# Four-stage gated cross-attention and mixture-of-experts kernel: a later store in one DMA queue, and products of a stage placed ahead of the work before them

## The reference, cut to what matters

```python
x = x + tanh(g_xattn[0]) * softmax_attention(_layernorm(x), ctx)      # stage A: 32 heads, masks
x = x + tanh(g_ffn[0])   * bitlinear_ffn(_layernorm(x))               # stage B: ternary weights
x = x + tanh(g_xattn[1]) * linear_attention(_layernorm(x), ctx)       # stage C: phi(q), phi(k), gate, Wo
x = x + tanh(g_ffn[1])   * moe(_layernorm(x))                         # stage D

# moe(x):
shared = (silu(x @ sw1.T) * (x @ sw2.T)) @ sw3.T                      # 2048 hidden
scores = sigmoid(x @ router_w.T)                                      # 8 experts, the top 2 of each token
h1, h2 = split(x @ w12[e].T); out_e = (silu(h1) * h2) @ w3[e].T       # 256 hidden in each expert
return shared + sum over the two experts of (weight * out_e)
```

## Time and profile before

| what | us |
| --- | --- |
| three runs: median (lowest to highest) | 1779.1 (1773.74 to 1786.65) |
| the profiled execution | 1774.64 |
| its span, first to last instruction | 1772.9 |
| PE busy in the span | 1594.1 (90%) |
| DVE, POOL, ACT busy | 967.4, 824.5, 711.1 |
| stage D's first PE product | at 1046.11 |
| routed stage on PE | 1497.17 to 1703.52 |
| mean granted TensorE clock | 0.969 of full speed |

### The profile page before, as it was taken

One profiled execution on the slowest core, in us unless ns is written; L12 is line 12 of the kernel. 1 busy time (PEld: TensorE's weight loads), 2 busy tenths in 40 slices (PEclk: granted clock), 3 DMA queues, 4 the chain that ended last, 5 costly groups with the idle time before them and its releaser, 6 DMA issues. The chain is left out here.

```text
span 1772.9 us, 29275 instructions
## 1 busy us (share of the span) xinstructions
PE 1594.1 (90%) x10826; PEld 829.7 (47%) x10826; DVE 967.4 (55%) x1947; ACT 711.1 (40%) x1311; POOL 824.5 (47%) x853
## 2 busy tenths in 40 slices
PE   4589999999848999979999979999999998888898
PEld 3246665665423444426565634444444443333343
DVE  5556666767547999834656443467543333111137
ACT  3178888888935556522233221211111111222211
POOL 2388887878843455433444245335433520111134
PEclk9899999999769999989999989999999999999999
DMA  5644544323414555443553437446544641565746
GB/s 165 163 103 108 114 94 109 95 66 67 115 27 91 120 116 108 83 89 70 96 123 81 93 84 161 99 101 135 127 102 101 154 88 36 147 158 145 153 134 192
DMA packets 453939, 195.68 MB, mean 110 GB/s; under 512 B 395484, under 2 KB 418270, under 8 KB 453800
## 3 DMA queue, kind: packets, MB, share of 16 engines
q1 hardware_dynamic: 448120, 175.19, 44.3%
q0 software_dynamic: 5680, 18.62, 4.1%
HBM read 77.17 MB, written 22.81 MB: 56 GB/s over the span
## 5 line engine op out<-in xcount | busy, mean ns | idle before, releaser
L1020 POOL TENSOR_TENSOR a_pl<-a_prob,a_ph 128x512 f16<-128x512 f32 x256 | 295.1, 1166 | 73.8 <-ACT a_prob L928 73.2
L1103 DVE TENSOR_REDUCE a_mx<-bank 128x2 f32<-128x512 f32 x256 | 173.0, 686 | 101.0 <-PE bank L652 99.2
L140 PE MATMUL bank<-XTh,d_whs 128*128 128x512 f16 x512 | 194.1, 379 | 3.2 <-PEq L89 2.3
L142 PE MATMUL bank<-XTh,d_wls 128*128 128x512 f16 x512 | 194.0, 379 | 0.0
L141 PE MATMUL bank<-XTl,d_whs 128*128 128x512 f16 x512 | 194.0, 379 | 0.0
L927 ACT ACTIVATE a_ph<-bank 128x512 f16<-128x512 f32 x256 | 153.9, 601 | 59.8 <-PE bank L672 32.0
L2225 POOL CAST d_cut<-d_raw 128x512 f16<-128x512 f32 x90 | 56.8, 631 | 228.3 <-DMA d_raw<-in_L_ffn_sw 147.9
L928 ACT ACTIVATE a_prob<-bank 128x512 f32<-128x512 f32 x256 | 154.3, 603 | 0.0
L2145 DVE TENSOR_TENSOR d_hid<-d_hid,bank 128x512 f32<-128x512 f32 x64 | 43.9, 686 | 175.4 <-PE bank L142 162.1
L2237 POOL DMA_INDIRECT e_x<-rows,d_who x39 | 37.1, 951 | 190.8 <-DMA e_xTl<-e_x 184.8
L2136 ACT ACTIVATE d_hid<-bank 128x512 f32<-128x512 f32 x64 | 38.2, 597 | 211.2 <-PE bank L142 211.2
(11 more groups left out here) (330 smaller groups left out, 3997.7 us busy)
## 6 DMA issues: line engine op xcount, KB each, us to landing
d_raw<-in_L_ffn_w SPq DMA_DIRECT2D x48, 256.0 KB, 3.0
d_raw<-in_L_ffn_sw SPq DMA_DIRECT2D x42, 256.0 KB, 3.0
made<-e_y SPq DMA_DIRECT2D x39, 256.0 KB
a_stage<-in_L_ffn_w_fc SPq DMA_DIRECT2D x32, 256.0 KB, 2.9
a_stage<-in_L_ffn_w_proj SPq DMA_DIRECT2D x32, 256.0 KB, 3.0
a_fbuf<-in_ctx SPq DMA_DIRECT2D x16, 256.0 KB, 3.3
rows<-f_cut SPq DMA_DIRECT2D x16, 256.0 KB, 2.5
out_x<-X SPq DMA_DIRECT2D x16, 256.0 KB
```

What stands on the lines that cost most here:

```text
L140: nc.tensor.matmul(out_ap, lhi, rhi, start=first, stop=False)
L142: return nc.tensor.matmul(out_ap, llo, rhi, start=False, stop=last_one)
L1020: nc.gpsimd.tensor_tensor(pl[:, n % NP, :], prob[:, n % 2, :], ph[:, n % NP, :], ALU.subtract).then_inc(ev["L"], 1)
L1103: nc.vector.tensor_reduce(mx[:, h, tt, half, 2 * (g % 4):2 * (g % 4) + 2], bank[BS + m % 2][:, :].rearrange("p (r k) -> p r k", r=2), AX_X ...
```

## The change

1. Stage C: after the last attention, PE waits for all six weight pieces and the first four tiles of x, makes the gate and up product of step 0 of stage D into banks 0 and 1 (not 4 and 5), and then the last output. In stage D step 0 has no gate and up any more; its signals are given by PE at the start, and ACT and DVE read banks 0 and 1 in step 0. `turn_router` moves between gate and up of step 1.
2. Routed stage, SP: store(j) is issued one tile later in the queue's order, behind turn(j + 3) instead of turn(j + 2).
3. Routed stage, start: PE's wait for `d_acc` (banks 0 to 3 read by DVE) moves from ahead of `routed_up(0)` to behind it.
4. Routed stage, end: the gate of step 56 moves ahead of the last `routed_down`. The down banks change places ((j + 1) % 2), so that bank 4 is free for it once y(37) is copied.
5. Last `pe_down`: a signal `d_end` after each of its four tiles, and `finish` waits for them one by one.

```diff
--- before.py
+++ after.py
@@ phase_c, tensor
+            for p in range(2 * CH // P + KC // 2):
+                turned(pe, "z", p)
+            for b in range(2):
+                turned(pe, "d", b, 0)
+                turned(pe, "d", b, 1)
+            for w in range(2):
+                for k in range(KC):
+                    last = env["three"](bank[w][:, :], env["whs"][:, 0, w, k, 0:P], env["wls"][:, 0, w, k, 0:P],
+                                        DTh[:, k, 0:BLK], DTl[:, k, 0:BLK], k == 0, k == KC - 1)
+                last.then_inc(c_shared, 1)
             output(B - 1)
+            pe.wait_ge(c_shared, 2)
@@ pe_gate (pe_up the same with d_hm)
-        if s:
+        if s > 1:
             pe.wait_ge(d_s, s)
@@ pe_down
+            if s == NS * SPC - 1:
+                last.then_inc(d_end, 1)
+        if s < NS * SPC - 1:
+            last.then_inc(d_dn, 1)
-        last.then_inc(d_dn, 1)
@@ act_step
-        nc.scalar.activation(hid[:, s % 2, :], bank[GATE][:, :], ACT.Silu).then_inc(d_s, 1)
+        nc.scalar.activation(hid[:, s % 2, :], bank[GATE if s else 0][:, :], ACT.Silu).then_inc(d_s, 1)
@@ dve_hid
-        ... bank[UP][:, :], ALU.mult).then_inc(d_hm, 1)
+        ... bank[UP if s else 1][:, :], ALU.mult).then_inc(d_hm, 1)
@@ phase_d, sync
-            for j in range(NT + 2):
+            for j in range(NT + 3):
...
-                if j >= 2:
-                    sp.wait_ge(e_y, j - 1)
-                    sp.dma_start(made[(j - 2) * P:(j - 1) * P, :], y[:, (j - 2) % YR, :]).then_inc(e_out[(j - 2) % YR], 16)
+                if j >= 3:
+                    sp.wait_ge(e_y, j - 2)
+                    sp.dma_start(made[(j - 3) * P:(j - 2) * P, :], y[:, (j - 3) % YR, :]).then_inc(e_out[(j - 3) % YR], 16)
@@ phase_d, tensor
             for p in range(NZ):
                 env["turned"](pe, "z", p)
+            pe.sem_inc(d_g, 1)
+            pe.sem_inc(d_u, 1)
@@ routed_down (routed_result the same)
-                    last = three(bank[EDN + j % 2][:, :]...
+                    last = three(bank[EDN + (j + 1) % 2][:, :]...
@@ the loop over s
                     pe.wait_ge(r_done, 2)
-                    pe.wait_ge(d_acc, LAST * BPC)
                     pieces_turned(pe, NQ - 1)
                     for j in range(NT):
                         routed_up(j)
                         if j:
                             routed_down(j - 1)
+                        else:
+                            pe.wait_ge(d_acc, LAST * BPC)
                         routed_turn(j)
+                    pe.wait_ge(e_y, NT - 1)
+                    pe_gate(pe, s)
                     routed_down(NT - 1)
                     pe.wait_ge(e_y, NT)
+                    pe_up(pe, s)
+                    continue
...
-                pe_gate(pe, s)
-                pe_up(pe, s)
-                if s == 0:
-                    turn_router()
+                if s:
+                    pe_gate(pe, s)
+                    if s == 1:
+                        turn_router()
+                    pe_up(pe, s)
@@ finish
-                dve.wait_ge(d_dn, (n + 1) * JC)
+                if n < NS * BPC - 1:
+                    dve.wait_ge(d_dn, (n + 1) * JC)
                 dve.wait_ge(c_x, TOP * TPB * (n % BPC + 1))
                 for tt in range(TPB):
+                    if n == NS * BPC - 1:
+                        dve.wait_ge(d_end, tt + 1)
```

More of the change, by code:

```diff
@@ L1670, in phase_c @@
     oTl = sb("c_oTl", [P, 2, KC, P], F16)
-    c_in, c_one = sem("c_in"), sem("c_one")
+    c_in, c_one, c_shared = sem("c_in"), sem("c_one"), sem("c_shared")
     names = ("K0", "K1", "V0", "V1", "Q0", "Q1", "G0", "G1",
@@ L2036, in phase_d @@
     y, YR = env["y"], 2
+    d_end = sem("d_end")
     d_g, d_u, d_s, d_hm, d_hi, d_lo, d_dn, d_acc = (sem("d_" + n) for n in (
@@ L2144, in dve_hid @@
         dve.wait_ge(d_s, s + 1)
-        nc.vector.tensor_tensor(hid[:, s % 2, :], hid[:, s % 2, :], bank[UP][:, :], ALU.mult).then_inc(d_hm, 1)
+        nc.vector.tensor_tensor(hid[:, s % 2, :], hid[:, s % 2, :], bank[UP if s else 1][:, :], ALU.mult).then_inc(d_hm, 1)
     def dve_low(dve, s):
@@ L2327, in routed_down @@
                     cols = slice(k * P, (k + 1) * P)
-                    last = three(bank[EDN + j % 2][:, :].rearrange("p (r c) -> p r c", r=KC), hh[:, j % 2, cols],
+                    last = three(bank[EDN + (j + 1) % 2][:, :].rearrange("p (r c) -> p r c", r=KC), hh[:, j % 2, cols],
                                  hl[:, j % 2, cols], hi, lo, k == 0, k == HC - 1)
@@ L2387, in routed_result @@
                     act.wait_ge(e_out[j % YR], 16 * (j // YR))
-                nc.scalar.activation(y[:, j % YR, :], bank[EDN + j % 2][:, :], ACT.Copy).then_inc(e_y, 1)
+                nc.scalar.activation(y[:, j % YR, :], bank[EDN + (j + 1) % 2][:, :], ACT.Copy).then_inc(e_y, 1)
             for s in range(NS * SPC):
```

## The result

The changed kernel takes 1750.95 us (median of 4 runs, 1747.62 to 1753.0) against 1776.45 (median of 4, 1773.74 to 1786.65) of the kernel before: a ratio of 0.9843 with a 95% interval of 0.9813 to 0.9874. That is 25.5 us less, where 31.5 were forecast. The same kernel, measured again later against its own runs of the kernel before, gave 0.9856 (0.983 to 0.9881), 28.0 us less. The profiled execution has a span of 1751.0 us, against 1772.9.

The account below looks back on a forecast made before the run. The kernel was taken as bound by TensorE, with gains only where PE stands still. Terms 24.4 + 4.6 + 0.7 + 0.5 + 1.2 + 0.1 = 31.5 us, off the 1779.1 median, gave 1748 us, range 1738 to 1762.

Parts of the forecast that it names:

- Routed slots: Routed stage, store one tile later: 37 slots on PE fall from 5.20 to 4.54 us each, 24.4 us less.
- Rival A: Routed stage: the DMA engines become the bound, the mean slot falls only to 4.9 us, time 1761; chance 0.13.
- The rule on packets served by turns: Each DMA engine serves queues with work by turns, a packet each; a routed-stage landing of 3.5 us could become 7.0.
- Rival B: Routed stage: the reorder does nothing, as the gather holds the transposes; other parts give 7 us, time 1772; chance 0.04.
- rival C: Routed stage: the store waits behind a late transpose; slower, 1798 us at slots of 5.9 us; chance 0.03.
- Start of the routed stage: Up(0) need not wait for the accumulators, so up(1) starts at 1498.75 instead of 1503.38: 4.6 us, up to 5.7.
- Stage C and start of D: 24 products of step 0 ahead of the third stage's last output: 0.5 us there, 1.2 us at the fourth's start.
- the two cases of the forecast: Fourth stage's start: 2.1 us gained, or 0.4 if the clock falls in PE's 2.7 us gap; 1.2 taken.
- Gate ahead of the last down: Routed stage's end: the gate covers PE's 1.29 us wait ahead of the last down, up(56) starts earlier: 0.7 us.
- Last down: Kernel's end, one signal per tile: DVE is late there, not PE, so only 0.1 us.
- I take nothing: Last chunk: combine gathers some 2.5 us later against PE, DVE's next hidden product about 2 us later; no cost taken.

Follow-up runs that it names:

- part 2 alone: Kernel before with only the store issued one tile later: 1755.49 us against 1774.03, ratio 0.9895.
- part 1 alone: Kernel before with only gate and up of step 0 ahead of the last output and the router's transposes moved: 1774.46 us against 1774.03, ratio 1.0001.
- without part 4: Changed kernel with gate and up of step 56 both behind the last routed down, down banks as before: 1747.36 us, ratio 0.9855.
- the hold: Changed kernel, POOL's combine gathers held to four ahead for the first 16, then six: 1747.02 us, ratio 0.9831; also without the gate ahead: 1747.89 us.

## Why the prediction was right, and where not

**Routed slots** (24.4 forecast, 23.3 found). The mechanism is as told. PE's waits for transposes are gone, the DMA share is 0.73 (0.77 forecast), and the transposes landed in time. (The window from which the 0.77 was worked out was denser than the stage: 0.67 there, 0.64 over 150 us, and 0.64 x 5.20 / 4.57 is 0.73.) Slots are 4.57 and not 4.54, since some gaps in front of an up product are 0.3 to 0.5 us and not 0.27. Rival A (DMA-bound) didn't come: gathers took up to 5.9 us to land instead of 4.7, with a median of 3.8 instead of 3.6, far from what would matter. The rule on packets served by turns, which the prediction took from the Trainium skill (DMA: Bandwidth & Descriptors, section "Queues, rings and completion order"), cannot be read off these runs; for the gathers, a doubling of the landings is not what they show, and the trace of the changed kernel gives no landing times for the transposes. Rival B fell with the run of the store order alone, rival C with the slots of 4.57 us and with the run of the store two tiles later, where no copy waited for a store.

**Start of the routed stage** (4.6 forecast, up to 5.7; 5.4 found). I kept 1.10 us as the read of an expert's number. It vanished: the first routed product follows the last shared one at the ordinary 0.22 us. My reading is that the read now runs behind the shared products and only came to light behind the wait; the run with the wait put back has the 4.2 us again, but no run takes the read apart. From up(0) to up(1) it took 4.84 us where I had 4.35.

**Stage C and start of D** (1.7 forecast, 1.6 found in the profiled run, 1.9 in the run of the part alone). The gap of 3.3 us and the one of 2.5 us are as forecast. The clock fell after the first, as taken, and for a shorter time after the second (some seven matmuls at 0.43 us), between the two cases of the forecast. With the router loads first the second gap moved to the wait for the low part of step 0, which the prediction had named as the next bound.

**Gate ahead of the last down** (0.7 forecast, 0.8 found): as told. **Last down** (0.1 forecast): DVE's finish follows its combines by 0.04 us instead of 0.10, and no run has this part alone.

**The combine gathers, "I take nothing"**: this step failed. What I had worked out did hold: DVE's product of step 57 came 10.6 us behind up(56) instead of 8.8, and PE didn't feel it. What I hadn't seen is that DVE's first finish or ACT's silu near it start late while POOL issues its first, unbroken burst of 14 gathers, 18.5 to 20.1 us behind the first of them. The kernel before already had it, hidden: 1.4 us late with no cost to PE. The two timelines showed it, but I read the finish's row as ordinary. With the gate ahead of the last down the burst starts 2.6 us later against PE, and the late finish reaches down(58). But the later burst isn't the whole cause: in the three kernels where it starts as early as before (part 2 alone, part 1 alone, without part 4) a late silu cost the chunk 0.8 to 2.2 us.

The traces say what DVE and ACT wait for: signals of PE. Four cases, all in us:

| kernel | product, its last matmul ends | signal raised | what starts |
| --- | --- | --- | --- |
| before | down(57), 1724.41 | 1725.79 | finish, 1725.81 |
| changed | down(57), 1698.45 | 1702.45 | finish, 1702.48 |
| without the gate ahead | gate(58), 1689.69 | 1696.12 | silu, 1696.15 |
| the same with the hold | gate(58), 1692.86 | 1692.88 | silu, 1692.90 |

In the third of them gate(58), up(58) and down(57) end 2.6 us apart, and their signals are raised within 0.26 us. From the first logits of stage D on, each of the fourteen traces records some 300 signals of PE. None ahead of the combine gathers is more than 0.3 us late; during the first burst and in the 3 us behind the start of its last gather the ten kernels without the hold have three to five late ones each, up to 6.4 us, and the four with it one of 0.5 us or none (one of these four has a signal 0.8 us late in the next series of gathers). No signal of ACT, DVE or POOL is late there. (The ends of matmuls are modelled by the profiler, but PE's next products start at their regular 0.216 us.)

Over the nine traces of kernels with some part of the change and without the hold, the chunk took 67.6 to 70.9 us, on average 1.8 us over the 66.8 of the one trace of before; with the hold on the first 16 it took 66.8 in all three kernels. That the burst causes the lateness is shown by the hold, though the break in the series and the smaller number of gathers (12 instead of 14) were not tried apart. How a burst on POOL keeps back PE's signals stays open. It wasn't tried to put DVE's low part ahead of the finish: nothing would then keep the next products out of banks that DVE still reads.

**The scatter.** The forecast by medians, 1748, lies between 1750.95 and 1747.91. That it is so near is in part luck. The saving was 3.5 to 6 us smaller than the 31.5 forecast, and the median of three that it was taken from, 1779.1, was 2.7 us higher than the one of four runs (1776.45) and 3 to 5 us higher than those of the later runs. The two errors stood against each other. By the traces the five parts gave 31.1 us against 31.5, and the chunk lost 0.9 to 4.1 that I had put at nothing.

## What to carry to other kernels

In this kernel a store at the end of the software pipeline had to stand in the DMA queue behind the transfers that an earlier stage of the pipeline needs before the stored value exists; the check for another kernel is to follow the last chain from one product to the next and count over how many tiles it closes (two before, three after: 5.20 to 4.57 us a tile). A wait on a shared resource belongs directly ahead of its first user: moved behind one product it gave 5.4 us, more than its visible 3.9, since the clock's fall went with it (behind the gap up(0) had some seven matmuls at 0.43 us, and without it none). And a late start that costs nothing in the profile of before, here 1.4 us on DVE, is worth a look, and so is the moment at which the signal was raised: a "remote" releaser in a program of one core was a late signal of a known engine.

## What the runs showed of the hardware

Signals of PE can come late while POOL issues gathers. With 14 gathers of 256 KB issued one after another, each 1.25 to 1.7 us behind the last, the signals of single PE products were raised up to 6.4 us behind the end of their last matmul, and an ACT or DVE instruction that stood waiting for one started 0.02 to 0.03 us after it. The profile then names no releaser or an impossible one. A break in the series (POOL idle for 0.8 to 1.3 us) and two gathers fewer left one signal late by 0.5 us in each of two kernels, and none in the other two.

The clock's fall after a gap is not a matter of the gap's length alone: after 2.23 us of idle time it fell in the changed kernel (0.66 over the stretch behind it), after 2.25 us at the same place of the program with the store two tiles later it stayed at 1.00.
